# Self-attention pair loop: query and key projection issued ahead of the output projection, rotation ahead of the residual

## Chip, cores and metric

The kernel runs on one core of a Trainium2 chip. The metric is the device time of one execution in microseconds (us), lower is better. An execution is the whole program of nine phases, and three executions of the kernel before were timed.

## What is computed

The reference applies four layers to `x` (64 sequences of 64 tokens, width 256) with a context `ctx_1024`. Layers 1 and 3 have the same form, with weights of their own, and open with the self-attention that the change is about. Cut to that part:

```python
def layer(hidden_states, ..., token_type_ids, position_ids, ln_in_w, v_qkv, l_qkv, v_dense, l_dense, ...):
    vm = expert_mask(token_type_ids)[..., None]          # token by token: v or l weights
    residual = hidden_states
    x = rms_norm(hidden_states, ln_in_w)
    mixed = jnp.where(vm, x @ v_qkv, x @ l_qkv)          # 256 -> 768
    q, k, v = jnp.split(mixed, 3, axis=-1)               # 16 heads of 16
    q, k = apply_rotary(q, k, position_ids, l)
    ctx = sdpa(q, k, v, causal=True)                     # per sequence of 64 tokens
    attn_out = jnp.where(vm, ctx @ v_dense, ctx @ l_dense)
    hidden_states = residual + attn_out
    ...                                                  # cross attention, gated feed forward
```

## The kernel before, in words

The program runs nine phases one after another: layer 0; self-attention, cross attention and gated feed forward of layer 1; latent attention and a GELU feed forward (layer 2); the same three again for layer 3. `self_attention(n, ...)` (L1010) is built twice, for n = 1 and n = 3. Each engine has its own instruction stream (`@block.tensor`, `@block.scalar`, `@block.gpsimd`, `@block.vector`, `@block.sync`), written out by hand, and the streams are held together by semaphores only. No scheduler moves anything: the order of the calls in a stream is the order on that engine.

Two kinds of unit run through a phase. A *tile* t (33 of them) is 128 tokens sorted so that a tile needs the weights of one kind only; tiles are projected to rows of query, key and value, which go to DRAM (`qkv_sorted`). A *pair* p (32 of them) is two whole sequences, 128 tokens, whose rows are gathered back from DRAM; rotation, scores, softmax, value product and output projection go by pairs. The loop over p works on tile t = p + 6 beside pairs p - 2 to p + 2, so one step of the loop is one tile and one pair. Tiles 0 to 5 are projected ahead of the loop. Steps p = 0 to 26 have a tile; steps 27 to 33 have none.

TensorE's stream in a step (L1229 to L1248):

- `scores(p)` (L1152): four causal-mask matmuls (L1159) and eight score matmuls (L1167).
- `probs_t(p - 1)` (L1173): eight transposes of the probabilities (L1181). The second four wait for the copy `qkt_copy` of pair p + 1 by ScalarE (L1179).
- `dense(p - 2)` (L1209): the output projection, six matmuls of 512 columns (L1215 to L1217) into PSUM `ps_b`.
- `proj_qk(t)` (L1127): the query and key projection, six matmuls of 512 columns (L1122 to L1124) into `ps_a`. `project` (L1117) first reads the tile's weight offset into a register with `value_load` (L1118, TENSOR_LOAD in the trace), checks it, and adds to it for each matmul.
- `pv(p - 1)` (L1185): 32 small matmuls (L1199). `x_t(t + 1)` (L1109): two transposes (L1114).
- `proj_v(t)` (L1134): the value projection, the same six matmuls with 256 columns, and a `value_load` of its own, into the first half of `ps_b`. Since `dense` of the same step has written the whole of `ps_b`, it waits until VectorE has read it: `res_ok` (L1139), raised by `residual(p - 2)`.
- `out_t(p - 1)` (L1203, two transposes, L1206) and `qk_t(p + 2)` (L1142, four transposes of rotated rows, L1149).

VectorE's stream in a step (L1479 to L1493): `softmax_front(p)` (two maxima at L374, two subtractions at L380), `residual(p - 2)` (L1451: waits for `dense` by `d_pe`, two instructions, L1453 and L1456, the second raises `res_ok`), `rope_products(p + 2)` (L1413: the rotation's three products, L1424 to L1426, of rows that a gather brought), `out_norm(p - 1)` (L1434: a reciprocal, L1437, and a product, L1441, after `pv`), `rope_sum(p + 2)` (L1431), `x_low(t + 1)` (L1410), `out_low(p - 1)` (L1447).

ScalarE evacuates: `pt_copy` (L1298), the softmax exponent (L388), `qk_rows(t)` (L1275, from `ps_a`), `x_high` (L1266), `stat_(t + 2)` (L1259, on rows of `x_in` that a DMA loads), `v_rows(t)` (L1280), `out_high` (L1305), `qkt_copy` (L1290). GpSimd spreads the keys (L1356), computes the norm factor (L1365, L1368) and issues the gathers (L1377); for n = 1 it also issues a scatter of words per step (L1383). SyncE issues, in this order, the store of tile t's rows once `v_ok` is raised (L1086), the load of tile t + 3 (L1078) and two copies of a pair's values (L1094).

Of the kernel before, what the change touches and what calls it, by code (L numbers as in the profile page):

```python
# [110 lines left out]
def build(nc, t):  # L111
    with ExitStack() as ctx:
# [183 lines left out]
        def has(p):  # L296

            return not isinstance(p, int) or 0 <= p < PAIRS
# [65 lines left out]
        def half(r):  # L364

            return slice(J * r, J * r + J)

        def softmax_front(dve, mx, probs, p, u):

            s3 = ps_s[:].rearrange("p (h k) -> p h k", k=S)  # L370
            pr = probs[:, u].rearrange("p (h k) -> p h k", k=S)
            for r in range(2):
                dve.wait_ge(s_pe.handle, s_pe.at(p, r + 1))
                nc.vector.tensor_reduce(mx[:, u, half(r)], s3[:, half(r)], op=ALU.max, axis=AX.X) \  # L374
                    .then_inc(max_ok.handle, 1)
            for r in range(2):
                dve.wait_ge(max_ok.handle, max_ok.at(p, r + 1))
                if r == 0 and pt_pe.due(p - 1):
                    dve.wait_ge(pt_pe.handle, pt_pe.at(p - 1))
                nc.vector.tensor_tensor(pr[:, half(r)], s3[:, half(r)],  # L380
                                        mx[:, u, half(r)].unsqueeze(2).broadcast_to([P, J, S]), ALU.subtract) \
                    .then_inc(sub_ok.handle, 1)
# [627 lines left out]
        def self_attention(n, loaded, load_next):  # L1010
            with ExitStack() as own:
# [54 lines left out]
                def is_tile(t):  # L1066
                    return 0 <= t < NT
# [39 lines left out]
                def _(pe):  # L1107
                    previous_done(pe)
                    def x_t(t):  # L1109
                        wait_tile(pe, t)  # L1110
                        if xlow_ok.due(t):
                            pe.wait_ge(xlow_ok.handle, xlow_ok.at(t))
                        for c in range(CH):
                            ins = nc.tensor.transpose(ps_t[:, c * P:c * P + P], x_in[:, t % X_SLOTS, c * P:c * P + P], ident)  # L1114
                        ins.then_inc(xt_pe.handle, 1)
# [11 lines left out]
                    def proj_qk(t):  # L1127

                        pe.wait_ge(xlow_ok.handle, xlow_ok.at(t + 1))
                        if evac_ok.due(t):  # L1130
                            pe.wait_ge(evac_ok.handle, evac_ok.at(t))
                        project(t, ps_a[:], 0, 2 * D).then_inc(qk_pe.handle, 1)
# [40 lines left out]
                    def probs_t(p):  # L1173
                        for r, bank in enumerate((ps_p, ps_d)):
                            pe.wait_ge(exp_ok.handle, exp_ok.at(p, r + 1))
                            if r == 0 and on_ok.due(p):
                                pe.wait_ge(on_ok.handle, on_ok.at(p))
                            if r == 1:
                                pe.wait_ge(qkt_ok.handle, qkt_ok.at(min(p + 3, PAIRS)))  # L1179
                            for j in range(4):  # L1180
                                ins = nc.tensor.transpose(bank[:, j * P:j * P + P],  # L1181
                                                          probs[:, p % 2, (4 * r + j) * P:(4 * r + j + 1) * P], ident)
                            ins.then_inc(pt_pe.handle, 1)
# [45 lines left out]
                    for p in range(PAIRS + 2):  # L1229
                        t = p + TILES  # L1230
                        if has(p):
                            scores(p)
                        if has(p - 1):
                            probs_t(p - 1)
                        if has(p - 2):
                            dense(p - 2)
                        if is_tile(t):
                            proj_qk(t)
                        if has(p - 1):
                            pv(p - 1)  # L1240
                        if is_tile(t + 1):
                            x_t(t + 1)
                        if is_tile(t):
                            proj_v(t)
                        if has(p - 1):
                            out_t(p - 1)
                        if has(p + 2):
                            qk_t(p + 2)  # L1248
# [157 lines left out]
                def _(dve):  # L1406
# [72 lines left out]
                    for p in range(PAIRS + 2):  # L1479
                        if has(p):  # L1480
                            softmax_front(dve, mx, probs, p, p % 2)
                        if has(p - 2):
                            residual(p - 2)
                        if has(p + 2):
                            rope_products(p + 2)
                        if has(p - 1):
                            out_norm(p - 1)
                        if has(p + 2):
                            rope_sum(p + 2)
                        if is_tile(p + TILES + 1):  # L1490
                            x_low(p + TILES + 1)
                        if has(p - 1):
                            out_low(p - 1)  # L1493
# [1337 lines left out]
```

## Time and profile before

| | us |
|---|---|
| three timed executions | 2355.1, 2352.7, 2341.13 |
| their median | 2352.7 |
| the profiled execution | 2359.21 |
| its span, first to last instruction | 2357.4 |
| PE (TensorE matmul) busy | 2121.8 (90%) |
| DVE (VectorE) busy | 1392.3 (59%) |
| ACT (ScalarE) busy | 1123.1 (48%) |
| POOL (GpSimd) busy | 819.0 (35%) |

The span was mapped by one execution under the hardware profiler. PE is the engine that computes matmuls, PEld the loading of its weights, PEldq or PEq its instruction sequencer, which handles register and semaphore instructions ahead of the array. Times in rows are from the span's start. "<-" behind an idle time names what ended it. In the timeline a matmul's start is recorded and its end is modelled, so consecutive matmuls overlap: the distance between starts is what one costs. In names, `ps_all` is all of PSUM, `pool_w` a large buffer shared by phases, and `s_` stands for the self-attention's own buffers of either layer.

The two self-attention loops lie at about 208 to 526 us (layer 1) and 1658 to 1929 us (layer 3).

### The profile page before, as it was taken

How to read it: one execution, taken by the hardware profiler on the slowest of the kernel's cores; microseconds unless marked ns; L12 is line 12 of the kernel's file. 1: busy time of each engine (PE TensorE's matmuls, PEld its weight loads, DVE VectorE, ACT ScalarE, POOL GpSimd, SP SyncE). 2: the span in 40 equal slices, each digit the busy share in tenths (PEclk: the TensorE clock that was granted, in tenths of full speed). 3: DMA queues.
4: the chain of work that ended last, by engine and by line, in shares of the span. 5: the costliest groups of instructions: out<-in, count | busy, mean ns of one | idle time of the engine just before them, and what ended most of it. 6: DMA issues, size and time to landing. Idle time of an engine off the chain costs nothing.

```text
span 2357.4 us, 63607 instructions
## 1 busy us (share of the span) xinstructions
PE 2121.8 (90%) x23904; PEld 1692.2 (72%) x23905; DVE 1392.3 (59%) x2863; ACT 1123.1 (48%) x2563; POOL 819.0 (35%) x1045
## 2 busy tenths in 40 slices
PE   8966888878997999699999987997899969979998
PEld 5644666655666999588888877996677746658997
DVE  6753666665774333466666656552788857763333
ACT  4753545436664333344443434444566537763332
POOL 1644545415652222111111111222444426652222
PEclk9977999988997999899999998999999989989999
DMA  7427777722003111300000001002444420011111
GB/s 227 127 68 102 113 109 109 105 45 83 27 29 105 58 58 53 112 2 3 2 3 2 2 2 47 26 20 80 139 130 130 127 89 20 29 42 52 59 59 36
DMA packets 105989, 155.11 MB, mean 66 GB/s; under 512 B 24099, under 2 KB 82288, under 8 KB 105616
## 3 DMA queue, kind: packets, MB, share of 16 engines
q0 software_dynamic: 16560, 55.23, 11.8%
q1 hardware_dynamic: 76288, 78.80, 11.4%
q10 hardware_dynamic: 12896, 17.64, 2.3%
q8 instruction: 174, 2.85, 0.6%
q14 instruction: 71, 0.58, 0.1%
HBM read 86.69 MB, written 56.28 MB: 61 GB/s over the span
## 4 chain that ended last, share of the span: by engine, by line
PE 75%; DVE 6%; DMA 4%; issue 3%; ACT 3%; ACTq 1%; another core or an unknown queue 1%; POOL 0%; SPq 0%; POOLq 0%; DVEq 0%
PE ps_all L2367 3%; PE ps_all L2365 3%; PE ps_all L2366 3%; DMA s_x_in<-x_sorted 3%; PE ps_all L1619 3%; PE ps_all L1591 3%; PE ps_all L1167 2%; PE ps_all L1181 2%; PE ps_all L1199 2%; PE ps_all L1122 2%; PE ps_all L2390 2%; PE ps_all L2392 2%; PE ps_all L2391 2%; PE ps_all L2375 2%; PE ps_all L1605 2%
## 5 line engine op out<-in xcount | busy, mean ns | idle before, releaser
L403 POOL TENSOR_TENSOR a_probs<-a_probs,a_sm 128x1024 f32<-128x1024 f32 x32 | 60.9, 1904 | 351.8 <-DVE a_sm L398 351.8
L1742 POOL TENSOR_TENSOR c_kx<-c_qkt,const 128x512 f32<-128x512 f32 x128 | 130.7, 1039 | 111.3 <-ACT c_qkt L1685 108.2
L1356 POOL TENSOR_TENSOR pool_w<-s_qkt,const 128x512 f32<-128x512 f32 x128 | 132.2, 1056 | 92.9 <-ACT s_qkt L1290 92.2
L2365 PE MATMUL ps_all<-f_wh,f_xh 128*128 x396 | 154.2, 389 | 4.9 <-DVE f_xl L2513 4.9
L2366 PE MATMUL ps_all<-f_wh,f_xl 128*128 x396 | 148.5, 375 | 0.0
L2367 PE MATMUL ps_all<-f_wl,f_xh 128*128 x396 | 148.3, 375 | 0.0
L2508 DVE SCALAR_TENSOR_TENSOR f_h<-ps_all,rstd,f_act_g 128x688 f32<-128x688 f32 x66 | 61.7, 934 | 142.0 <-PE ps_all L2367 128.8
L2086 ACT ACTIVATE self_w<-ps_all,a_q_bias 128x256 f32<-128x256 f32 x128 | 53.7, 471 | 189.5 <-PE ps_all L1930 189.5
L1122 PE MATMUL ps_all<-s_wh,s_xh 128*128 x264 | 102.3, 388 | 27.0 <-issue 15.4
L2390 PE MATMUL ps_all<-f_dh,f_hh 128*128 x396 | 116.9, 295 | 4.0 <-DVE f_hl L2523 4.0
L2429 ACT ACTIVATE f_act_g<-ps_all,rstd 128x688 f32<-128x688 f32 x66 | 55.2, 837 | 131.6 <-PE ps_all L2367 131.6
L2434 ACT ACTIVATE f_hh<-ps_all 128x768 fp32r<-128x768 f32 x66 | 53.6, 812 | 133.2 <-PE ps_all L2375 133.2
L374 DVE TENSOR_REDUCE s_mx<-ps_all 128x8 f32<-128x512 f32 x128 | 82.5, 685 | 55.9 <-PE ps_all L1167 47.6
L1693 ACT ACTIVATE c_pt<-ps_all 128x512 f32<-128x512 f32 x128 | 69.4, 595 | 93.5 <-PE ps_all L1605 93.5
L2392 PE MATMUL ps_all<-f_dl,f_hh 128*128 x396 | 111.5, 282 | 0.0
L2391 PE MATMUL ps_all<-f_dh,f_hl 128*128 x396 | 111.3, 281 | 0.0
L1792 DVE TENSOR_REDUCE c_mx<-ps_all 128x8 f32<-128x512 f32 x128 | 82.4, 686 | 44.3 <-PE ps_all L1591 44.1
L1298 ACT ACTIVATE s_pt<-ps_all 128x512 f32<-128x512 f32 x128 | 71.4, 596 | 76.7 <-PE ps_all L1181 75.3
L2523 DVE TENSOR_TENSOR f_hl<-ps_all,f_hh 128x768 fp32r<-128x768 f32 x66 | 63.2, 958 | 65.5 <-ACT f_hh L2434 65.5
L1365 POOL TENSOR_TENSOR s_power<-s_power,eps 128x1 f32<-128x1 f32 x66 | 13.5, 204 | 240.6 <-ACT s_junk L1259 238.5
L1123 PE MATMUL ps_all<-s_wl,s_xh 128*128 x264 | 93.3, 353 | 0.0
L1181 PE MATMUL ps_all<-const,s_probs 128*128 128x128 f32 x512 | 75.5, 288 | 19.6 <-ACT s_qkt L1290 19.5
(338 smaller groups left out, 6981.9 us busy)
## 6 DMA issues: line engine op xcount, KB each, us to landing
qkv_sorted<-pool_w SPq DMA_DIRECT2D x66, 392.0 KB
pool_w<-pool_w SPq DMA_DIRECT2D x128, 68.0 KB
s_x_in<-x_sorted SPq DMA_DIRECT2D x66, 128.0 KB
f_x_in<-x_sorted SPq DMA_DIRECT2D x66, 128.0 KB, 2.0
x_res<-x_sorted SPq DMA_DIRECT2D x66, 128.0 KB, 2.1
x_sorted<-x_res POOLq DMA_DIRECT2D x1, 4224.0 KB, 17.4
l_rows<-in_x SPq DMA_DIRECT2D x32, 128.0 KB
x_res<-in_x SPq DMA_DIRECT2D x32, 128.0 KB
```

What stands on the lines that cost most here:

```text
L374: nc.vector.tensor_reduce(mx[:, u, half(r)], s3[:, half(r)], op=ALU.max, axis=AX.X) \
L1122: nc.tensor.matmul(out, high, wh[:, w_at], start=(c == 0), stop=False)
L1123: nc.tensor.matmul(out, high, wl[:, w_at], start=False, stop=False)
L1181: ins = nc.tensor.transpose(bank[:, j * P:j * P + P], probs[:, p % 2, (4 * r + j) * P:(4 * r + j + 1) * P], ident)
L1356: ins = nc.gpsimd.tensor_tensor(kx[:, p % 2, c], qkt[:, p % 2, 2 + c].rearrange("p (b k) -> p b k", b=2).unsqueeze(2) .broadcast_to([P, 2, ...
L1742: ins = nc.gpsimd.tensor_tensor(kx[:, p % 2, b], qkt[:, p % 2, 1, b * S:b * S + S].unsqueeze(1).broadcast_to([P, RH, S]), const[:, C_H8X:C ...
L2365: nc.tensor.matmul(bank, x_high, wh[:, w_at], start=(c == 0), stop=False)
L2366: nc.tensor.matmul(bank, x_low, wh[:, w_at], start=False, stop=False)
L2367: ins = nc.tensor.matmul(bank, x_high, wl[:, w_at], start=False, stop=(c == CH - 1))
L2390: nc.tensor.matmul(bank, high, dh[:, w_at], start=(m == 0), stop=False)
L2391: nc.tensor.matmul(bank, low, dh[:, w_at], start=False, stop=False)
L2392: ins = nc.tensor.matmul(bank, high, dl[:, w_at], start=False, stop=(m == IC - 1))
```

## The change

Two calls change places, one on each of two engines, in both layers. On TensorE, `proj_qk(t)` is called before `dense(p - 2)`. On VectorE, `rope_products(p + 2)` is called before `residual(p - 2)`. No instruction is added or removed, and every wait stays with its call.

```diff
@@ TensorE, loop over p
                             probs_t(p - 1)
+                        if is_tile(t):
+                            proj_qk(t)
                         if has(p - 2):
                             dense(p - 2)
-                        if is_tile(t):
-                            proj_qk(t)
                         if has(p - 1):
                             pv(p - 1)
@@ VectorE, loop over p
                             softmax_front(dve, mx, probs, p, p % 2)
+                        if has(p + 2):
+                            rope_products(p + 2)
                         if has(p - 2):
                             residual(p - 2)
-                        if has(p + 2):
-                            rope_products(p + 2)
                         if has(p - 1):
                             out_norm(p - 1)
```

TensorE in step p = 2 of layer 1, from the last probability transposes on, in the kernel before. The names in brackets are the semaphores that an instruction waits for: `evac_ok` and `xlow_ok` guard `proj_qk`, `v_ok` and `o_ok` guard `dense`.

```order
L1181 MATMUL ps_all<-const,s_probs 128x128 [waits qkt_ok,exp_ok]
L1181 MATMUL ps_all<-const,s_probs 128x128 x3
L1215 MATMUL ps_all<-s_oh,s_oth 128x512 [waits v_ok,o_ok]
L1216 MATMUL ps_all<-s_ol,s_oth 128x512
L1217 MATMUL ps_all<-s_oh,s_otl 128x512
L1215 MATMUL ps_all<-s_oh,s_oth 128x512
L1216 MATMUL ps_all<-s_ol,s_oth 128x512
L1217 MATMUL ps_all<-s_oh,s_otl 128x512
L1118 TENSOR_LOAD off_qkv [waits evac_ok,xlow_ok]
L1118 ISA x2
L1122 ISA
L1122 MATMUL ps_all<-s_wh,s_xh 128x512
```

The same place in the kernel after the change:

```order
L1181 MATMUL ps_all<-const,s_probs 128x128 [waits qkt_ok,exp_ok]
L1181 MATMUL ps_all<-const,s_probs 128x128 x3
L1118 TENSOR_LOAD off_qkv [waits evac_ok,xlow_ok]
L1118 ISA x2
L1122 ISA
L1122 MATMUL ps_all<-s_wh,s_xh 128x512
```

The register load and its checks moved from behind the six matmuls of `dense` to right behind the transposes. The end of that stretch, after the change (between these rows and the ones above stand the other five matmuls of `proj_qk` and the first five of `dense`):

```order
L1217 MATMUL ps_all<-s_oh,s_otl 128x512
L1199 MATMUL ps_all<-pool_w,s_pt 64x17 [waits v_in1,o_ok,qkv_in1,pt_ok]
L1199 MATMUL ps_all<-pool_w,s_pt 64x17 x31
L1114 MATMUL ps_all<-const,s_x_in 128x128 [waits xlow_ok,xs_in0]
L1114 MATMUL ps_all<-const,s_x_in 128x128
L1118 TENSOR_LOAD off_qkv [waits res_ok,v_ok]
L1118 ISA x2
L1122 ISA
L1122 MATMUL ps_all<-s_wh,s_xh 128x256
```

The last matmul of `dense` is now the one directly ahead of `pv`; before, the last of `proj_qk` stood there. The register load of `proj_v` is unmoved, with its wait for `res_ok`.

VectorE in a step, before:

```order
L380 TENSOR_TENSOR s_probs<-ps_all,s_mx 128x512 [waits max_ok]
L1453 SCALAR_TENSOR_TENSOR s_part<-ps_all,vm,x_res 128x256 [waits d_pe]
L1456 SCALAR_TENSOR_TENSOR x_res<-ps_all,vm,s_part 128x256 [waits mix_ok]
L1424 TENSOR_TENSOR s_roped<-pool_w,rope 128x512 [waits qkt_pe,qkv_in0]
L1425 TENSOR_TENSOR s_roped<-pool_w,rope 128x32x8
L1426 TENSOR_TENSOR s_roped<-pool_w,rope 128x32x8
L1437 RECIPROCAL s_inv<-ps_all 128x16 [waits pv_pe]
```

and after:

```order
L380 TENSOR_TENSOR s_probs<-ps_all,s_mx 128x512 [waits max_ok]
L1424 TENSOR_TENSOR s_roped<-pool_w,rope 128x512 [waits qkt_pe,qkv_in0]
L1425 TENSOR_TENSOR s_roped<-pool_w,rope 128x32x8
L1426 TENSOR_TENSOR s_roped<-pool_w,rope 128x32x8
L1453 SCALAR_TENSOR_TENSOR s_part<-ps_all,vm,x_res 128x256 [waits d_pe]
L1456 SCALAR_TENSOR_TENSOR x_res<-ps_all,vm,s_part 128x256 [waits mix_ok]
L1437 RECIPROCAL s_inv<-ps_all 128x16 [waits pv_pe]
```

The residual's two instructions moved behind the three products, next to the reciprocal.

## Rows read from the trace of the kernel before

**Rows 1.** The page, busy time, share of the span and instructions.

```profile
PE 2121.8 (90%) x23904; PEld 1692.2 (72%) x23905; DVE 1392.3 (59%) x2863; ACT 1123.1 (48%) x2563; POOL 819.0 (35%) x1045
```

**Rows 2.** Windows: stretch, length, busy per engine (instructions), clock, DMA share, GB/s.

```profile
219.00:471.00 252.00, 216.88 (x2945) 164.79 (x2944) 166.05 (x349) 125.56 (x273) 125.89 (x149) 0.97 0.74 106
1672.80:1880.40 207.60, 202.34 (x2954) 159.90 (x2954) 168.34 (x349) 124.79 (x271) 94.33 (x122) 1.00 0.42 130
```

**Rows 3.** Timeline, TensorE, one step of layer 3 (start, length, instruction).

```profile
1822.44 0.41 PE L1159 MATMUL ps_all<-causal_b,ident_b 64*64 64x512 bf16 x4
...
1825.79 0.40 PE L1217 MATMUL ps_all<-s_oh,s_otl 128*128 128x512 f32 x1
...
1827.17 0.39 PE L1124 MATMUL ps_all<-s_wh,s_xl 128*128 x1
1827.49 1.12 PE L1199 MATMUL ps_all<-pool_w,s_pt 64*64 64x17 f32 x64
...
1829.16 0.38 PE L1122 MATMUL ps_all<-s_wh,s_xh 128*128 x1 [0.18 <-issue]
...
1830.72 0.41 PE L1159 MATMUL ps_all<-causal_b,ident_b 64*64 64x512 bf16 x4
```

**Rows 4.** Timeline, VectorE, the same step.

```profile
1824.96 1.28 DVE L380 TENSOR_TENSOR s_probs<-ps_all,s_mx 128x512 f32<-128x512 f32 x2
1826.23 0.48 DVE L1453 SCALAR_TENSOR_TENSOR s_part<-ps_all,vm,x_res 128x256 f32<-128x256 f32 x1
1826.75 0.48 DVE L1456 SCALAR_TENSOR_TENSOR x_res<-ps_all,vm,s_part 128x256 f32<-128x256 f32 x1
1827.15 0.68 DVE L1424 TENSOR_TENSOR s_roped<-pool_w,rope 128x512 f32<-128x512 f32 x1
...
1828.68 0.26 DVE L1437 RECIPROCAL s_inv<-ps_all 128x16 f32<-128x16 f32 x1 [0.18 <-PE ps_all L1199]
```

**Rows 5.** Instructions of L1118 and of L1139 in that step: ns min/median/max, first and last start.

```profile
L1118 PEldq TENSOR_LOAD <-off_qkv x2: 301/510/720, 1823.5 to 1828.4; - x2
L1139 PEldq EVENT_SEMAPHORE  x1: 51/51/51, 1828.3 to 1828.3; - x1
```

**Rows 6.** Timeline, TensorE, step p = 1 of layer 3, which has no output projection.

```profile
1665.89 0.41 PE L1159 MATMUL ps_all<-causal_b,ident_b 64*64 64x512 bf16 x4
...
1669.37 0.40 PE L1124 MATMUL ps_all<-s_wh,s_xl 128*128 x1
```

**Rows 7.** Timelines, TensorE and VectorE, layer 3, step p = 29.

```profile
1902.70 0.40 PE L1217 MATMUL ps_all<-s_oh,s_otl 128*128 128x512 f32 x1
...
1903.14 0.48 DVE L1453 SCALAR_TENSOR_TENSOR s_part<-ps_all,vm,x_res 128x256 f32<-128x256 f32 x1 [0.70 <-PE ps_all L1217]
```

**Rows 8.** Timelines, ScalarE and TensorE, ahead of layer 1's loop: projections that waited.

```profile
174.06 0.68 ACT L1275 ACTIVATE pool_w<-ps_all,s_factor 128x512 f32<-128x512 f32 x1
175.62 0.49 PE L1122 MATMUL ps_all<-s_wh,s_xh 128*128 x1 [1.18 <-ACT pool_w L1275]
...
177.46 0.45 ACT L1280 ACTIVATE pool_w<-ps_all,s_factor 128x256 f32<-128x256 f32 x1
178.71 0.38 PE L1122 MATMUL ps_all<-s_wh,s_xh 128*128 x1 [1.21 <-ACT pool_w L1280]
```

**Rows 9.** All starts of L1118 in steps 2 to 26 of layer 3.

```profile
L1118 PEldq TENSOR_LOAD <-off_qkv x50: 298/439/771, 1673.9 to 1878.0; - x50
```

**Rows 10.** Layer 1's loop: what ended idle time before L1259, L1181, L1149 (us, times).

```profile
  DMA s_x_in<-x_sorted: 30.9, 11
...
  ACT s_qkt L1290: 19.5, 13
...
  DVE s_roped L1431: 3.4, 11
```

**Rows 11.** Timeline, VectorE, layer 1, steps p = 27 and p = 29.

```profile
482.16 0.48 DVE L1453 SCALAR_TENSOR_TENSOR s_part<-ps_all,vm,x_res 128x256 f32<-128x256 f32 x1 [0.52 <-PE ps_all L1217]
...
500.74 0.48 DVE L1453 SCALAR_TENSOR_TENSOR s_part<-ps_all,vm,x_res 128x256 f32<-128x256 f32 x1 [0.27 <-PE ps_all L1217]
```

## The prediction

> **What bounds the kernel now.** I read the page first: TensorE is busy for 90% of the span and no other engine for more than 59% [rows 1]. An average over nine phases says little about two of them, so next come windows over the steps that have both a tile and an output projection, p = 2 to 26. Both windows are cut at about those 25 steps. In layer 3 they take 207.6 us, 8.30 us each, with TensorE busy for 202.3 of them at full clock; in layer 1 nearly the same work takes 252 us with a DMA share of 0.74 [rows 2]. So the two loops have different limits, and a change has two prices.
>
> The timeline of one step of layer 3 shows TensorE without a gap, except 0.18 us ahead of the value projection that is put down to issue [rows 3]. The step runs from 1822.44 to 1830.72, 8.28 us. In what follows I count from its start: last matmul of the output projection starts at 3.35, last matmul of the query and key projection at 4.73, `pv` at 5.05, value projection at 6.72. VectorE in the same step ends the softmax subtraction at 3.80, and goes through the residual from 3.79 to 4.79, the products from 4.71, and the reciprocal at 6.24, where it waited only 0.18 us for `pv` [rows 4]. Its idle time costs nothing here.
>
> The third view is of the sequencer. In that step two register loads start, at 1.1 (0.72 us long, for the query and key projection) and at 6.0 (0.30 us, for the value projection), and the wait for `res_ok` at L1139 is passed at 5.9 [rows 5]. The first is taken while the array still has the output projection ahead of it, so it is hidden; the second is what makes the 0.18 us of issue. Before the change `res_ok` is raised at 4.79 and asked for at 5.9: 1.1 us to spare. This slack is what the change spends.
>
> **The change part by part.** Nothing is added or removed, so I price only positions. TensorE does the same twelve matmuls in the other order; VectorE the same five instructions.
>
> *TensorE: the register load loses its cover.* The first projection matmul now comes straight after the transposes. Step p = 1 has that very order, since it has no output projection: its sixth matmul of 512 columns starts 3.48 us after the step's start [rows 6]; in a step with the output projection first, the sixth starts at 3.35 [rows 3]. The cost is 0.13 us per step. Below, it could be nothing where the load is as short as 0.30 us; above, where the transposes themselves have waited, the load starts only after the release, and of a load-to-matmul time that I price below at 0.75 the four transposes hide about a third. I put that at 0.5 us for each such step, 13 of them in layer 1 [rows 10].
>
> *The residual comes later, and the value projection waits for it.* The last matmul of the output projection takes the slot at 4.73, plus 0.13: 4.86. Where VectorE stood waiting for it, the residual began 0.44 us after that matmul's start (1902.70 to 1903.14) [rows 7]: 5.30. VectorE is free by then: from 3.79 the three products take what they took before, 1827.15 to the end of the group, about 1.3 us, to some 5.1. The residual lasts 1.00 us (1826.23 to 1827.23) [rows 4]: `res_ok` at 6.30. The sequencer asks for it at 5.9 + 0.13 = 6.0, so the 1.1 us of slack has become a wait. Behind the waiting instruction stand the register load, the six value matmuls, the transposes of `out_t` and `qk_t`, and the next step's scores; ScalarE's `v_rows`, the statistics' successor loads on SyncE and GpSimd's gathers hang on them. From a release to the first matmul the trace has two cases: 174.74 to 175.62, 0.88 us, where two semaphores guard the load, and 177.91 to 178.71, 0.80 us, where one does [rows 8]. `proj_v` has two, as the first case has: 6.30 + 0.88 = 7.18. Before, the matmul started at 6.72. The step is 0.46 us longer, the 0.13 included.
>
> Nothing later in the step takes this back. The reciprocal waits for `pv` (6.24, now 6.37) and VectorE leaves the residual at 6.30, so `out_norm` and `rope_sum` end 0.13 us later while TensorE comes to them 0.46 us later. ScalarE's evacuation of `ps_a` can start 1.4 us earlier, but nothing waits for it: the next `proj_qk` wants it 5 us later. The rotation's input is wanted 0.9 us earlier than before; in layer 3 VectorE never waited for it in these 25 steps, of which [rows 4] is a typical one, so this costs nothing.
>
> *The Trainium skill on the load.* The 50 loads of these steps range from 0.298 to 0.771 us [rows 9]. The page DMA: Bandwidth & Descriptors of the Trainium skill, section Latency and other measured facts, gives a register load a floor of about 600 ns. By that floor the value projection's load would take 0.30 us more than its row shows, a step 0.76 us more than before instead of 0.46, and 25 steps 19 us instead of 11.5, an estimate from that page. Here the load at the value projection took 0.30 [rows 5] and half of all 50 stay below 0.44, so the measurement decides and the rule gets no chance of its own.
>
> *Layer 3.* 25 steps at 0.46 us: +11.5 us.
>
> *Layer 1.* ScalarE waited 11 times, 30.9 us in all, for the DMA that loads a tile [rows 10]. There the step is load, statistics, `v_rows`, store, next load, and TensorE's 0.46 us only shortens its own wait. In the other 14 steps I charge it: 14 x 0.46 = +6.4 us. The bounds are 0 (all covered) and 25 x 0.46 = +11.5. The extra 0.5 us behind a late release, 13 steps, has bounds 0 and +6.5; I take 0, since these waits lie in the steps that the DMA sets.
>
> *Steps without a tile.* From p = 27 TensorE's order is as it was. On VectorE the products now fill a wait for the output projection where there was one: 0.52 and 0.27 us in layer 1 [rows 11], 0.70 in layer 3 [rows 7]; VectorE sets those steps, so all of it is gained: -1.5 us. The remaining three of six such steps had no wait there and give nothing.
>
> *Sum.* +11.5 + 6.4 - 1.5 = +16.4 us. On the profiled execution that is 2359.2 to 2375.6; it lies 6.5 us above the median of the timed runs, so for these 2352.7 + 16.4 = 2369 us, 0.7% longer.
>
> **Rivals.**
>
> *A: the residual is in time.* If the sequencer reaches the wait later than I think, or takes the release faster, only the uncovered load is left: 50 x 0.13 - 1.5 = +5 us, 2358 us. For it: VectorE's end and the sequencer's question are 0.3 us apart in my sum, less than one instruction. Against it: the matmul needs the load and the checks after the release, 0.8 us in both cases that the trace has [rows 8].
>
> *B: layer 1 hides nothing.* The load of tile t + 3 is issued only after `v_rows(t)`, which now comes 0.46 us later in every step; if the DMA's latency is simply added behind it, all 25 steps pay, and the late releases 0.5 us more: 11.5 + 11.5 + 6.5 - 1.5 = +28 us, 2381 us. For it: the loop of load and store runs through TensorE's value projection. Against it: that projection was long done in the 11 steps in which ScalarE waited for the load.
>
> *C: faster.* VectorE gains more than TensorE loses. The mechanism sits at `qk_t`: in layer 1 TensorE waited 11 times, 3.4 us, for the rotation's sum [rows 10], since residual and products both stood between the output projection and it. With the products done early these go, as do the 1.5 us of the tail, and, if steps without DMA waits lose nothing, the time is 2352.7 - 4.9 = 2348 us. It decides if `res_ok` is raised before the sequencer asks, that is if the residual starts 0.3 us earlier than I have it and the register load is hidden after all. Against it stands the count of 5.30, and a step of layer 3 in which TensorE has nothing to gain.
>
> **How the numbers follow.** My forecast has 0.62, with its own range of 2360 to 2378 us; A 0.13, B 0.17, C 0.08. The range reaches from a little below A to just above B: 2353 to 2383 us. About 1% is what a measurement of this kernel can tell from no change, 2329 to 2376 us here. Above 2376 lie B and the upper edge of my own case: 0.22. Below 2329 nothing that I can name: 0.02. Within: 0.76.
>
> **What would show it.** In layer 3 the steps should last 8.74 us, the 25 of them 219 us. TensorE should be idle before L1122 of the value projection for some 0.5 us, released by L1456 on VectorE rather than by issue, and about 0.1 us before the first L1122 of the step. L1453 should wait for L1217. In layer 1 the same wait should stand in the undisturbed steps, and fewer or shorter waits at L1181. Wrong would be: steps of 8.3 or 8.4 us in layer 3 (A or C), or a loop in layer 1 that grew by more than 15 us (B), or steps in which L1149 waits longer for L1431 than now.

## The result, and the profile after

After the change the kernel takes 2366.32 us (median of 7 runs, 2361.93 to 2372.12), before it 2352.08 (7 runs on the same chip). The ratio is 1.0072 with an interval of 1.0049 to 1.0094: slower by 16.9 us, 11.5 to 22 by the interval. The profiled execution after the change has a span of 2365.9 us. The one before had 2357.4, and its own time was about 7 us above the median of these runs, so the two spans differ by less, 8.5 us, than the medians do. Whole times are therefore compared by ratios here, and traces only stage by stage. The ratios are of executions in the chip's usual state; one execution of a later kernel, before_reuse_sum, took 4039.55 us where the other eleven took 2348 to 2359, and its ratio leaves it out.

The page, busy time and share, to be read beside [rows 1]:

```profile
PE 2120.5 (90%) x23904; PEld 1693.3 (72%) x23905; DVE 1398.6 (59%) x2863; ACT 1119.6 (47%) x2563; POOL 818.7 (35%) x1045
```

Nothing here tells of the change: TensorE is busy for 1.3 us less than before, in a program that takes longer. The windows over steps 2 to 26 (columns as in [rows 2]), first layer 1 before and after, cut at exactly these steps, then layer 3 after:

```profile
223.56:476.49 252.93, 217.78 (x2950) 165.68 (x2950) 166.98 (x349) 125.29 (x271) 124.78 (x147) 0.97 0.75 107
224.98:483.53 258.55, 222.36 (x2950) 169.09 (x2949) 173.31 (x350) 124.07 (x274) 124.77 (x148) 0.94 0.74 105
1672.00:1888.70 216.70, 202.72 (x2953) 159.97 (x2954) 168.61 (x349) 122.07 (x271) 94.34 (x122) 1.00 0.41 125
```

In layer 3 the 25 steps grew from 207.6 us [rows 2] to 216.7, +9.1, with 202 to 203 us of busy TensorE at the same clock: 8.7 of it is idle time of TensorE. In layer 1 they grew by 5.6, and there it is the other way round: TensorE's busy time grew by 4.6 us, at a granted clock of 0.94 instead of 0.97, and its idle time by 1.0. One step of layer 3, TensorE's timeline, as in [rows 3]:

```profile
1828.07 0.41 PE L1159 MATMUL ps_all<-causal_b,ident_b 64*64 64x512 bf16 x4
...
1829.34 1.09 PE L1181 MATMUL ps_all<-const,s_probs 128*128 128x128 f32 x8
1830.18 0.48 PE L1122 MATMUL ps_all<-s_wh,s_xh 128*128 x1
...
1832.80 0.40 PE L1217 MATMUL ps_all<-s_oh,s_otl 128*128 128x512 f32 x1
...
1834.18 0.44 PE L1114 MATMUL ps_all<-const,s_x_in 128*128 128x128 f32 x2
1835.13 0.38 PE L1122 MATMUL ps_all<-s_wh,s_xh 128*128 x1 [0.51 <-issue]
...
1836.69 0.41 PE L1159 MATMUL ps_all<-causal_b,ident_b 64*64 64x512 bf16 x4
```

And VectorE's in the same step, to be held against [rows 4]:

```profile
1831.79 0.68 DVE L1424 TENSOR_TENSOR s_roped<-pool_w,rope 128x512 f32<-128x512 f32 x1
...
1832.72 0.41 DVE L1426 TENSOR_TENSOR s_roped<-pool_w,rope 128x256 f32<-128x256 f32 x1
1833.24 0.48 DVE L1453 SCALAR_TENSOR_TENSOR s_part<-ps_all,vm,x_res 128x256 f32<-128x256 f32 x1
1833.75 0.48 DVE L1456 SCALAR_TENSOR_TENSOR x_res<-ps_all,vm,s_part 128x256 f32<-128x256 f32 x1
```

The step lasts 8.62 us instead of 8.28. Counted from its start: the output projection's last matmul starts at 4.73, the residual at 5.17, its second instruction ends at 6.16, and the value projection starts at 7.06, 0.90 us after that end. Before, it started at 6.72. The 0.34 us that the step grew is this one shift.

The label of the wait says "issue", which invites a wrong reading. The sequencer shows what it is. Instructions of L1139 (the wait for `res_ok`) and of L1118 (the register load) in this step, ns min/median/max, first and last start:

```profile
L1139 PEldq EVENT_SEMAPHORE  x1: 51/51/51, 1834.3 to 1834.3; - x1
L1118 PEldq TENSOR_LOAD <-off_qkv x2: 297/478/658, 1829.0 to 1834.4; - x2
L1118 PEldq SEQ_ASSERT  x2: 18/18/18, 1830.0 to 1835.0; - x2
```

VectorE's last instruction ends at 1834.23, the wait is passed at 1834.3, 6.2 us into the step instead of 5.9 [rows 5], the load starts at 1834.4, the last check of its value at 1835.0, the matmul at 1835.13. So the sequencer waits for the residual, and the engine behind it waits for load and checks, which come last, so that the row says issue. In one step, p = 26, the row names L1456: no transposes of a next tile run meanwhile, and the idle time there is 0.89 us. By the trace's own times, to the hundredth, the wait is passed 5.87 us into the step before and 6.21 after: 0.34 us later, which is what the step grew.

The chain of waits of TensorE sums this up. Layer 3, steps 2 to 26, what it waited for, us in total, times, longest; the kernel before:

```profile
PE ps_all L1122 <- issue: 5.3, 25, 0.4
```

and after:

```profile
PE ps_all L1122 <- issue: 13.1, 24, 0.6
PE ps_all L1122 <- DVE x_res L1456: 0.9, 1, 0.9
```

That is 14.0 - 5.3 = 8.7 of the 9.1 us. Layer 1, the same view, before:

```profile
PE ps_all L1181 <- ACT s_qkt L1290: 19.5, 13, 4.0
PE ps_all L1206 <- DVE s_on L1441: 6.3, 3, 3.5
PE ps_all L1122 <- issue: 5.4, 26, 0.5
```

and after:

```profile
PE ps_all L1122 <- issue: 19.6, 35, 1.0
PE ps_all L1181 <- ACT s_qkt L1290: 11.0, 8, 2.1
PE ps_all L1206 <- DVE s_on L1441: 2.6, 3, 1.1
PE ps_all L1122 <- DVE x_res L1456: 1.8, 1, 1.8
```

In layer 1 the waits at the projections grew by 21.4 - 5.4 = 16.0 us, and those at L1181 and L1206 shrank by 8.5 + 3.7 = 12.2. Most of the new idle time was taken out of idle time that was there. That the tile's DMA stands behind those waits is argued from ScalarE, which makes the copy that L1181 waits for: it waited 8 times, 23.9 us, for the tile, where it was 11 times, 30.9 us [rows 10]. What lowered the granted clock from 0.97 to 0.94 is not shown. It is 0.95 over the same steps of a kernel that has the old order in layer 1 (layer3_only, below), so the clock varies without the change as well.

The register load of the query and key projection has become a cost of its own: where the transposes ahead of it were released late, TensorE stands again behind them. One of these places in layer 1, TensorE's timeline after the change:

```profile
239.10 0.63 PE L1181 MATMUL ps_all<-const,s_probs 128*128 128x128 f32 x4 [1.99 <-ACT s_qkt L1290]
240.36 0.79 PE L1122 MATMUL ps_all<-s_wh,s_xh 128*128 x1 [0.63 <-issue]
```

Ten of the 36 waits at L1122 stand at the query and key projection, 0.26 to 0.68 us each and 5.7 us in all, eight of them directly behind a wait at L1181; before, six output projection matmuls stood there and the load lay beside them.

The steps from p = 27 on, by the starts of L1159: steps 27 to 29 of layer 3 last 25.98 us instead of 26.92, those of layer 1 24.5 instead of 28.4, where before one wait of 0.9 us at L1167 and a lower clock (0.88, after 0.93) stood as well.

### The profile page after: what moved, and what is told of

Read it like the earlier page. It is cut to its first block, busy times and chain, and to the rows that moved or that the text cites. A ratio compares the mean times of both kernels' runs of the same rounds, so it can differ in the third digit from the quotient of the medians.

```text
span 2365.9 us, 63607 instructions
## 1 busy us (share of the span) xinstructions
PE 2120.5 (90%) x23904; PEld 1693.3 (72%) x23905; DVE 1398.6 (59%) x2863; ACT 1119.6 (47%) x2563; POOL 818.7 (35%) x1045
## 3 DMA queue, kind: packets, MB, share of 16 engines
q1 hardware_dynamic: 76288, 78.80, 11.5%
## 4 chain that ended last, share of the span: by engine, by line
PE 73%; DVE 6%; DMA 6%; issue 4%; ACT 3%; ACTq 1%; POOL 0%; another core or an unknown queue 0%; SPq 0%; POOLq 0%; DVEq 0%
DMA s_x_in<-x_sorted 4%; PE ps_all L2366 3%; PE ps_all L2365 3%; PE ps_all L2367 3%; PE ps_all L1619 3%; PE ps_all L1591 3%; PE ps_all L1167 2%; PE ps_all L1199 2%; PE ps_all L1181 2%; PE ps_all L1122 2%; PE ps_all L2390 2%; PE ps_all L2392 2%; PE ps_all L2391 2%; PE ps_all L2375 2%; PE ps_all L1635 2%
## 5 line engine op out<-in xcount | busy, mean ns | idle before, releaser
L1356 POOL TENSOR_TENSOR pool_w<-s_qkt,const 128x512 f32<-128x512 f32 x128 | 132.0, 1055 | 89.9 <-ACT s_qkt L1290 89.2
L1122 PE MATMUL ps_all<-s_wh,s_xh 128*128 x264 | 107.1, 406 | 51.4 <-issue 37.6
L1122 PEld LDWEIGHTS ps_all<-s_wh,s_xh 128*128 128x128 f32 x264 | 52.7, 199 | 74.5 <-issue 70.6
L1124 PE MATMUL ps_all<-s_wh,s_xl 128*128 x264 | 94.4, 357 | 0.0
```

The source lines that it names most:

```text
L1122: nc.tensor.matmul(out, high, wh[:, w_at], start=(c == 0), stop=False)
L1124: ins = nc.tensor.matmul(out, low, wh[:, w_at], start=False, stop=(c == CH - 1))
L1356: ins = nc.gpsimd.tensor_tensor(kx[:, p % 2, c], qkt[:, p % 2, 2 + c].rearrange("p (b k) -> p b k", b=2).unsqueeze(2) .broadcast_to([P, 2, ...
```

## The experiments

All kernels compute the full result. "L3 step" is the median of the 25 steps with a tile and an output projection in layer 3, from the profiled execution; the ratio is that of the timed runs to the kernel before on the same chip.

| kernel | ratio [95%] | L3 step, us | 25 steps, us |
|---|---|---|---|
| before | 1 | 8.29 | 207.5 |
| after | 1.0072 [1.0049, 1.0094] | 8.63 | 216.6 |
| dve_only | 1.0032 [1.0010, 1.0054] | 8.44 | 211.1 |
| pe_only | 1.0153 [1.0125, 1.0181] | 9.30 | 232.6 |
| after_vload | 1.0019 [0.9996, 1.0042] | 8.33 | 208.3 |
| before_oneload | 1.0000 [0.9984, 1.0016] | 8.37 | 210.1 |
| layer3_only | 1.0039 [1.0010, 1.0068] | 8.63 | 216.4 |
| layer1_only | 1.0017 [0.9994, 1.0039] | 8.29 | 207.2 |
| after_reuse | 0.9998 [0.9978, 1.0018] | 8.30 | 207.0 |
| before_reuse | 0.9992 [0.9970, 1.0014] | 8.19 | 204.7 |
| after_later | 1.0187 [1.0140, 1.0234] | 9.04 | 230.4 |
| before_reuse_sum | 1.0008 [0.9987, 1.0029] | 8.27 | 206.8 |

My theory: `res_ok` is raised later than the sequencer asks for it, and what stands behind the wait (a load, its checks) costs TensorE the difference. Its rivals: the uncovered load at the query and key projection makes the loss; layer 1 makes it; the residual is in time.

**dve_only and pe_only: one half of the change each.**

```diff
dve_only, on the kernel before, VectorE's order:
-                        if has(p - 2):
-                            residual(p - 2)
                         if has(p + 2):
                             rope_products(p + 2)
+                        if has(p - 2):
+                            residual(p - 2)
pe_only, on the kernel before, TensorE's order:
-                        if has(p - 2):
-                            dense(p - 2)
                         if is_tile(t):
                             proj_qk(t)
+                        if has(p - 2):
+                            dense(p - 2)
```

> VectorE's half of the change alone: the rotation's products ahead of the residual, TensorE's order as in the kernel before. Theory (the value projection starts 0.90 us after res_ok, since the register load stands behind the wait): the residual then runs from 5.06 to 6.06 us of the step, so the value projection starts at 6.95 instead of 6.72 and the 25 full steps of layer 3 last 8.51 to 8.53 us, 213 us in all; the time is 4 to 9 us over the kernel before. Rival (only TensorE's exchanged order costs, by an uncovered register load): steps of 8.29 us and the time of the kernel before, or 1 to 3 us less for the steps without a tile.

> TensorE's half alone: query and key projection ahead of the output projection, VectorE's order as in the kernel before. Theory: the residual starts with the end of the output projection at 5.16 us of the step and res_ok comes at 6.15, as after the whole change, but the products follow only then, the rotation's sum ends near 8.66 instead of 7.55, and TensorE now waits at L1149 for it: steps of 9.2 us in layer 3 and 15 to 35 us over the kernel before in all. Rival (the register load alone): 8.6 us per step as after the whole change, 14 us over before, with no wait at L1149.

dve_only: TensorE's order is untouched, yet the step grew by 0.15 us. VectorE and TensorE in order of time:

```profile
1838.73 0.48 DVE L1456 SCALAR_TENSOR_TENSOR x_res<-ps_all,vm,s_part 128x256 f32<-128x256 f32 x1
...
1840.11 0.38 PE L1122 MATMUL ps_all<-s_wh,s_xh 128*128 x1 [0.34 <-issue]
```

The residual ends at 1839.21, 0.90 us ahead of the matmul and 5.99 us into a step that began at 1833.22. The wait at L1139 is passed at 6.02 by the trace's own times, where before it was at 5.87: 0.15 us later, and the step is 0.15 us longer. I had expected steps of 8.51 to 8.53 us and got 8.44, since the residual came 0.07 us earlier than I had it. The whole is 7.5 us longer by the ratio (2.4 to 12.7), within the 4 to 9 expected.

pe_only costs more than the whole change. Its VectorE and TensorE in order of time:

```profile
1833.90 0.48 DVE L1456 SCALAR_TENSOR_TENSOR x_res<-ps_all,vm,s_part 128x256 f32<-128x256 f32 x1
1834.31 0.68 DVE L1424 TENSOR_TENSOR s_roped<-pool_w,rope 128x512 f32<-128x512 f32 x1
...
1835.29 0.38 PE L1122 MATMUL ps_all<-s_wh,s_xh 128*128 x1 [0.53 <-issue]
...
1836.20 0.68 DVE L1431 TENSOR_TENSOR s_roped<-s_roped 128x512 f32<-128x512 f32 x1
...
1836.34 0.44 PE L1206 MATMUL ps_all<-const,s_on 128*128 128x128 f32 x2
...
1836.93 0.66 PE L1149 MATMUL ps_all<-const,s_roped 128*128 128x128 f32 x4 [0.16 <-DVE s_roped L1431]
```

The value projection starts 0.91 us after the residual, as in after; then the products, which now come behind the residual, push `out_norm` and `rope_sum` back, and TensorE waits a second time, for them: 9.30 us a step, +1.0, and +36 us in all (29 to 43), a little above the 9.2 us and the 15 to 35 that I had expected. So the uncovered load is not needed for a loss (dve_only has none and loses), and VectorE's half of the change is what keeps TensorE's half from costing twice as much.

**after_vload: the load ahead of the wait.** Only the register load of the value projection moves ahead of the two waits.

```diff
                     def proj_v(t):
...
+                        at = offset(t)
                         if v_ok.due(t):
                             pe.wait_ge(v_ok.handle, v_ok.at(t))
```

> The kernel after the change, with one move: the value projection reads its weight offset into the register ahead of its waits for v_ok and res_ok instead of behind them. Theory: res_ok still comes at 6.15 us of the step, but from there the matmul is 0.2 us away instead of 0.90, so the load's own end sets the start, at 6.5 to 6.7; the steps of layer 3 fall from 8.62 to 8.1 to 8.3 us and the time to that of the kernel before or 0 to 6 us below it. Rival (the residual itself is too late, by the exchanged projections): the start stays within 0.1 us of 7.06 and the steps stay at 8.5 to 8.62.

The residual ends 6.16 us into a step that starts at 1832.49, as late as in after:

```profile
1838.17 0.48 DVE L1459 SCALAR_TENSOR_TENSOR x_res<-ps_all,vm,s_part 128x256 f32<-128x256 f32 x1
...
1839.23 0.38 PE L1124 MATMUL ps_all<-s_wh,s_xh 128*128 x1 [0.19 <-issue]
```

It ends at 1838.65 and the matmul starts 0.58 us later, with 0.19 us of idle time, nearly what before had [rows 3]. The step is back at 8.33 us, though the load at the query and key projection stands where the change put it, so that load costs 0.04 us of the 0.34 at most. The rest was paid because load and checks, 0.75 us from the load's start to the matmul, stood behind its wait. Whole: 1.0019, some 12 us less than after. Both lie a little above my expectation: the step by 0.03 us, and the whole at 4.5 us over before (-0.9 to 9.9), where I had 0 to 6 below it.

**before_oneload, after_reuse, before_reuse: one load for two uses.** Both projections of a tile read the same register value. before_oneload takes it at the head of the step, the two others at the query and key projection.

```diff
before_oneload:
+                        if is_tile(t):
+                            at = offset(t)
before_reuse and after_reuse, in proj_qk; proj_v takes the same at:
+                        at = offset(t)
+                        project(t, ps_a[:], 0, 2 * D, at).then_inc(qk_pe.handle, 1)
```

> The kernel before, in its own order, with one register load per tile, read at the head of the step ahead of all waits and used by both projections. Theory: the 0.18 us of issue before the value projection goes, steps of layer 3 fall from 8.29 to 8.11 us (4.5 us in all), the tiles ahead of both loops save some 0.4 us for each wait that had a load behind it, and the time is 5 to 12 us below the kernel before. Rival (the load is no cost once TensorE is the bound): steps of 8.29 us, the same time.

> The kernel after the change with one register load per tile, at its place in the query and key projection, and no load in the value projection. Theory: nothing of 0.7 us stands behind res_ok any more; the value projection follows the transposes at 6.45 to 6.55 us of the step, TensorE is then held at the rotation's transposes by VectorE (sum done at 7.55 to 7.6) and steps of layer 3 last 8.15 to 8.25 us, 0 to 10 us below the kernel before. Rival (the late residual itself costs): 8.4 us or more per step.

> The kernel before with the same single load, which there has the output projection to hide it. Theory: the 0.18 us ahead of the value projection goes, but VectorE's sum at 7.55 us holds the rotation's transposes, so steps of layer 3 last 8.17 to 8.25 us instead of 8.29, and 2 to 8 us go in all. Rival (the load at the step's head was the loss in before_oneload only by chance, and VectorE holds nothing): 8.11 us.

before_oneload missed its expectation, with a step of 8.37 instead of 8.11 us and a ratio of 1.0000 (5 to 12 us less had been expected). TensorE:

```profile
1838.59 0.66 PE L1151 MATMUL ps_all<-const,s_roped 128*128 128x128 f32 x4
1839.51 0.41 PE L1161 MATMUL ps_all<-causal_b,ident_b 64*64 64x512 bf16 x4 [0.27 <-issue]
```

The gap ahead of the value projection is gone, and a new one stands ahead of the scores. `qk_t` had to wait for VectorE, so the sequencer reached the load only at 1838.6, and 0.60 us of transposes don't cover it. Layer 1's late releases look the same: a load that is reached only with the transposes ahead of it.

With the load at the query and key projection the old gap goes. after_reuse, VectorE and TensorE of a step that starts at 1831.33:

```profile
1837.02 0.48 DVE L1462 SCALAR_TENSOR_TENSOR x_res<-ps_all,vm,s_part 128x256 f32<-128x256 f32 x1
...
1837.44 0.44 PE L1114 MATMUL ps_all<-const,s_x_in 128*128 128x128 f32 x2
1837.75 0.38 PE L1126 MATMUL ps_all<-s_wh,s_xh 128*128 x1
```

From the release (1837.50) to the matmul it is 0.25 us without a load, against 0.90 with one: this is the price of what stands behind the wait, 0.65 us. In this step the transposes of L1114 reach up to the matmul, so 0.25 might only be a bound; in step p = 26, which has no such transposes, TensorE was idle for 0.24 us, the row names the residual, and it is 0.25 again. The change with this repair equals the kernel before (0.9998). Here the uncovered load does cost something: in ten steps it took 0.56 to 0.60 us and the first projection matmul starts at 2.11, in the other fifteen it took 0.72 to 0.86 us and that matmul starts 0.06 to 0.23 us later. The steps last 8.20 us and 8.26 to 8.43 us, 8.28 in the mean, a little over the 8.15 to 8.25 that I had expected. before_reuse has 8.19 us in every step, as expected; its 0.9992 as a whole (0.9970 to 1.0014) can't tell the 2 to 8 us that I had expected from nothing.

**layer3_only and layer1_only: where the loss lies.** The new order in one layer's loop alone.

```diff
layer3_only (layer1_only has n == 1 here and n == 3 below), VectorE likewise:
-                        if is_tile(t):
+                        if n == 3 and is_tile(t):
                             proj_qk(t)
                         if has(p - 2):
                             dense(p - 2)
+                        if n == 1 and is_tile(t):
+                            proj_qk(t)
```

> The change in layer 3 alone, layer 1 in the old order. In the changed kernel's profile the 25 full steps of layer 3 grew by 9.1 us and the steps behind them shrank by 1. Theory: +7 to +9 us on the kernel before, and layer 3's steps at 8.62 us. Rival (the loops hide nothing and nothing else differs): the same, so this run is the yardstick for the next.

> The change in layer 1 alone. Theory (steps in which ScalarE waits for the tile's DMA hide TensorE's later value projection): +3 to +6 us on the kernel before, less than with layer 3 alone. Rival B of the prediction (layer 1 hides nothing, and the register load behind the late releases is added): +9 us or more.

Layer 3 alone costs 1.0039, +9.2 us (2.4 to 16.0), and its loop 216.4 us as in after. Layer 1 alone costs 1.0017, +4.0 (-1.4 to +9.2), which is not clear of no change; the interval just reaches the 9 us that I had set as rival B's least, and leaves out the 11.5 + 6.5 = 18 us of B's own sum for this layer. The two add up to 13 of 16.9 us, within their intervals. The loop of layer 1 took 258.2 and 258.5 us in the two traces with the new order, and 252.9 and 245.9 in the two with the old one; from execution to execution it varies as much as the change moves it, so the split within layer 1 stays a rough one.

**after_later: the slope.** If the residual's end decides, making VectorE late must make the step late. One product of 512 elements more, into a spare buffer that nothing reads, ahead of the residual:

```diff
+                            if is_tile(p + TILES):
+                                rope_again(p + 2)
                         if has(p - 2):
                             residual(p - 2)
```

> The kernel after the change, with one product of 512 elements more on VectorE ahead of the residual in every step that has a tile; its result goes to a spare buffer that nothing reads. In after, VectorE is free of the rotation's products some 4.95 us into a step of layer 3 and starts the residual at 5.16, when the output projection is done. With 0.6 to 0.7 us more it starts the residual at about 5.6. Theory (the value projection waits for the residual's release, and VectorE's end decides): the release comes 0.4 to 0.5 us later, the projection's first matmul starts 0.9 us behind it as before, a step of layer 3 lasts 9.05 to 9.15 us instead of 8.63, 25 steps 227 to 229 us, and the whole is 10 to 20 us above after. Rival (the wait is put down to issue because the register load and its checks make it, not the release): VectorE has time to spare, the step stays at 8.6 to 8.7 us and the whole within 3 us of after.

VectorE and TensorE of a step that starts at 1839.62:

```profile
1844.61 0.68 DVE L1432 TENSOR_TENSOR s_spare<-rope 128x512 f32<-128x512 f32 x1
...
1845.73 0.48 DVE L1462 SCALAR_TENSOR_TENSOR x_res<-ps_all,vm,s_part 128x256 f32<-128x256 f32 x1
...
1847.11 0.38 PE L1123 MATMUL ps_all<-s_wh,s_xh 128*128 x1 [0.72 <-issue]
```

VectorE's product of 0.6 us delays the residual by 0.43 us (it ends 6.59 us into the step, at 1846.21), the matmul starts 0.90 later again, and the step is 9.04 us (9.05 to 9.15 expected): 0.41 for 0.43. In other steps the row now names the releaser; TensorE's waits in layer 3:

```profile
PE ps_all L1123 <- DVE x_res L1462: 20.7, 22, 1.0
```

The rival falls. Of the 25 steps 20 had this length; five were 0.7 to 1.1 us longer, 4.3 us in all, at a lower granted clock in three places. The whole is 1.0187, about 27 us over after, above the 10 to 20 I had expected, with an interval of some 12 us to each side.

**before_reuse_sum: what is left in before_reuse.** There TensorE's `qk_t` waits for the rotation's sum in each step. So VectorE's sum goes ahead of the normalisation.

```diff
on before_reuse, VectorE's order, the sum ahead:
-                        if has(p - 1):
-                            out_norm(p - 1)
...
+                        if has(p - 1):
+                            out_norm(p - 1)
```

> The kernel before the change, with one register load for each tile, taken at the query and key projection and used again by the value projection, and on VectorE the rotation's sum ahead of the normalisation of the output. Without the second change the step of layer 3 lasted 8.19 us, and the transposes of the rotation waited for the sum in it. Theory (that wait is all that is left over the matmuls themselves, 8.09 us): steps of 8.08 to 8.14 us in layer 3, 25 of them 202 to 204 us; the normalisation comes 0.7 us later, and the transpose of the output that waits for it comes ahead of the rotation's in TensorE's order, so this can eat what is won. Rival (the normalisation is then what is late): TensorE waits at the transposes of the output instead, steps of 8.3 us or more, 25 of them over 207 us. Against before, whole: 0.995 to 0.999 by the theory, 1.000 or above by the rival.

VectorE and TensorE ahead of the next step's scores:

```profile
1836.40 0.42 DVE L1447 TENSOR_TENSOR s_on<-ps_all,s_inv 128x256 f32<-128x256 f32 x1
...
1836.88 0.44 PE L1212 MATMUL ps_all<-const,s_on 128*128 128x128 f32 x2 [0.23 <-DVE s_on L1447]
```

The rival was right: the wait moved one group ahead, to the normalisation, and grew from 0.14 to 0.22 us; 8.27 us a step. No version that I ran beats the kernel before by more than its measurement is uncertain.

## Why the prediction was right, and where its terms were off

The time was forecast at 2369 us, +16.4, and measured at 2366.3, +16.9 by the ratio. The mechanism stood as stated. That the two figures lie 0.5 us apart is luck: the ratio's own interval is 11.5 to 22 us, and the pieces that were measured add up to less than the forecast: to 10 us by the two traces (9.1 - 0.9 in layer 3, 5.6 - 3.9 in layer 1), to 13 by the ratios of layer3_only and layer1_only. The terms:

- **The value projection waits for the residual.** Right. It is shown by after_later (0.41 us a step for 0.43 us of lateness), by dve_only (0.15 for 0.15) and by after_vload and after_reuse, which take the load from behind the wait. The 0.88 us from release to matmul measured 0.90. Where I looked for L1456 as the releaser in the rows, all steps of layer 3 but one say issue, because the load ends last; the sequencer's rows tell.
- **The uncovered load, +0.13 us a step: this term was too large.** The first projection matmul starts 2.10 us into the step, where the output projection's did before. I had taken the 0.13 from step p = 1, whose load is longer than any of the 50 in [rows 9] (0.81, first row below). At its new place the load took 0.59 to 0.74 us, 0.63 in the median, where it was 0.57 to 0.77 and 0.73 before: it is just covered. In 23 of the 25 steps the matmul starts at 2.1; in the two with the longest loads (0.74 and 0.73), which also started 0.09 and 0.15 us later, it is 0.14 and 0.20 us late. (Seven other steps are 0.1 us longer between the residual's release and its matmul, which I did not follow up.) So the residual starts at 5.17 and not 5.30, the projection at 7.06 and not 7.18, and the step is 8.62 and not 8.74. The term is not nothing in general: with the loads of 0.72 to 0.86 us in after_reuse it was 0.06 to 0.23 us.
- **Layer 3:** +9.1 instead of +11.5 us, by that term.
- **Layer 1:** +6.4 was forecast, with bounds of 0 and 11.5; the traces show +5.6 between the two loops, the ratio of layer1_only +4.0. The number is near, but not for the reason given. I had charged 0.46 us in 14 steps and nothing in the others. The rows show 16.0 us more at the projections, close to the 18 of rival B, and 12.2 less at L1181 and L1206; 1.0 us of idle time is left in the sum, and the other 4.6 us are busy time at a lower clock, which I had no term for. The extra behind a late release, which I put at 0, is there, 5.7 us in ten places, near its upper bound of 6.5; since TensorE's idle time as a whole grew by 1.0 us, it too was mostly paid out of waits that were there. How much exactly I could not separate.
- **Steps without a tile:** -1.5 forecast; -0.9 in layer 3, where I had 0.7, by the traces. In layer 1 I had 0.8, and the traces show -3.9, with a wait of 0.9 us and a clock in it that I did not tie to the change. The term may have been too small there: steps 27 to 29 of layer 1 last 24.5 to 28.2 us in the six traces in which the products come ahead of the residual and 27.4 to 33.0 in the six in which they come behind it.
- **Rival A** (in time) fell: the overrun is 0.3 us, as in my sum. **B** fell with layer1_only and with the ratio of the whole: what it charges is there, but most of it is given back. **C** fell too. Its 3.4 us, 11 times [rows 10], were a misreading: that row counts the idle time of the weight loads ahead of the matmuls as well. Asked for the matmuls alone, it says 0.5 us, 3 times, before and 0.3, 2 times, after (second and third row below), so C had 0.5 us to win there and not 3.4.

The load of step p = 1 of layer 3 before, and what ended idle time of TensorE's matmuls before L1149 in layer 1's loop, before and after:

```profile
L1118 PEldq TENSOR_LOAD <-off_qkv x1: 814/814/814, 1666.9 to 1666.9; - x1
...
  DVE s_roped L1431: 0.5, 3
...
  DVE s_roped L1431: 0.3, 2
```

The Trainium skill's page DMA: Bandwidth & Descriptors, section Latency and other measured facts, puts a register load at no less than about 600 ns. After the change the 25 loads at the value projection in layer 3 took 0.296 to 0.311 us, so here the rule does not hold; at the query and key projection, 0.59 to 0.74, it fits, but in pe_only, at the same place, 24 of the 25 took 0.38 to 0.53. With 600 ns at both, the estimate from that page was 19 us for layer 3, and 9.1 was measured.

## What to carry to other kernels

Before an instruction that releases a wait is moved back, find the time at which the waiting sequencer asks for it: until then lateness is free, beyond it every tenth of a microsecond is paid in each step where the waiting engine sets the pace, as in layer 3. In layer 1, where it also waited for other things, three quarters of it came out of those waits. Whatever stands between the wait and the first instruction that needs it (a register load and its checks, 0.65 us here) is added to every late release, so take such loads ahead of the wait or once for several uses, but behind enough queued work to cover them. Two reorderings should be priced together: TensorE's alone would have cost 36 us here, VectorE's 7.5, both 16.9.

## What I had not expected of the hardware

The same register load, from the same table, takes 0.30 us at the value projection and 0.57 to 0.77 at the query and key projection, in every one of the 25 steps of layer 3 in both kernels. The other traces widen the second figure to 0.30 to 0.86: 0.38 to 0.53 in pe_only (24 of 25), 0.33 to 0.63 in before_reuse. It is not that an entry is fast when it is read a second time: in before_oneload each entry is read once, at the step's head, in 0.30 us. What ran beside the loads differs. These are windows over the long and the short load of one step of after (columns as in [rows 2]; the DMA share is counted by the packets that start in the window, so that a short one can read above 1):

```profile
1829.05:1829.70 0.65, 0.65 (x11) 0.37 (x4) 0.31 (x1) 0.00 (x0) 0.65 (x1) 1.00 1.20 396
1834.38:1834.68 0.30, 0.24 (x2) 0.00 (x0) 0.27 (x2) 0.03 (x1) 0.00 (x0) 1.00 0.02 0
```

The DMA engines moved 396 GB/s beside the long one and nothing beside the short one, and GpSimd was busy throughout the one (with L1356) and idle in the other. Whether one of these makes the difference was not tried.

The granted clock fell inside a loop in which TensorE was idle once in each step. In after, with 0.5 to 0.6 us of it in a step, the window over 25 steps of layer 3 shows 1.00. In pe_only, with 0.77 us in a step, in more than one piece, it shows 1.00 over 25 steps too:

```profile
1679.28:1911.92 232.64, 213.30 (x2950) 159.86 (x2949) 166.56 (x350) 126.84 (x271) 94.33 (x122) 1.00 0.37 116
```

In after_later, with 0.94 us in one piece, it fell in three places to 0.50, the lower of its two levels (1.2 instead of 2.4 GHz), for 3.4 us each, every time 0.2 to 0.5 us behind the end of such an idle time. Windows over the first 13 steps and over the first of the three places:

```profile
1675.20:1792.80 117.60, 105.42 (x1536) 83.25 (x1534) 93.32 (x195) 64.07 (x144) 52.77 (x66) 1.00 0.40 121
1800.80:1804.20 3.40, 3.40 (x27) 2.62 (x29) 0.58 (x2) 1.41 (x3) 1.17 (x2) 0.50 0.38 118
```

The two steps around that place took 19.7 us instead of 2 x 9.04, 1.6 more, with the same instructions. Five of the 25 steps were longer in this way, 4.3 of the 27 us. That the longer idle time is the reason is only argued: nearly all other steps had the same 0.94 us at full clock.
